# Cross-attention on one core: a GpSimd subtraction stops waiting for VectorE's rotation add, and a VectorE step moves one slot ahead

## The reference

```python
h = rmsnorm(x, norm_w)
q = rope((h @ Wq.T).reshape(B, Td, H, D), 0, D)
kv = (ctx @ Wkv.T).reshape(B, Te, 2, H, D)
k, v = rope(kv[:, :, 0], 0, D), kv[:, :, 1]
attn = softmax(einsum('bqhd,bkhd->bhqk', q, k) * D ** -0.5)
out = x + einsum('bhqk,bkhd->bqhd', attn, v).reshape(B, Td, d) @ Wo.T
```

## Time and profile before

| | |
|---|---|
| Time, median of 3 runs | 1491.78 us (1489.89 to 1495.62) |
| Profiled execution, its own time | 1495.62 us |
| Its span | 1493.8 us |
| Mean granted TensorE clock | 0.96 of full |
| Busy: PE, DVE, ACT, POOL | 87%, 78%, 60%, 59% |
| Longest groups on POOL and DVE | L1073 128 x 3096 ns; L1117 128 x 1936 ns |
| DMA packets | 310827, 148 GB/s |

### The profile page before, as it was taken

One profiled execution on the slowest core, in us unless ns is written; L12 is line 12 of the kernel. 1 busy time (PEld: TensorE's weight loads), 2 busy tenths in 40 slices (PEclk: granted clock), 3 DMA queues, 4 the chain that ended last, 5 costly groups with the idle time before them and its releaser, 6 DMA issues.

```text
span 1493.8 us, 34244 instructions
## 1 busy us (share of the span) xinstructions
PE 1297.5 (87%) x11592; PEld 715.1 (48%) x11592; DVE 1169.0 (78%) x1696; ACT 899.6 (60%) x1202; POOL 887.7 (59%) x738
## 2 busy tenths in 40 slices
PE   2787766799899999999899999999999999989997
PEld 1443332455455554555455555455545555545554
DVE  3755664788787888888788888888888888879874
ACT  2622333666566766766676666676667666756552
POOL 1234553567565666666666666666666666666551
PEclk9999896899999999999999999999999999999999
DMA  3433254677777777777777776777777777786642
GB/s 130 126 109 108 65 155 83 126 149 161 140 157 154 167 163 166 165 166 164 167 164 163 165 166 165 167 164 164 159 162 154 164 162 164 159 167 141 148 114 85
DMA packets 310827, 221.09 MB, mean 148 GB/s; under 512 B 230416, under 2 KB 284816, under 8 KB 302576
## 3 DMA queue, kind: packets, MB, share of 16 engines
q1 hardware_dynamic: 307984, 215.29, 64.1%
q10 hardware_dynamic: 2784, 5.05, 0.9%
HBM read 92.16 MB, written 43.65 MB: 91 GB/s over the span
## 4 chain that ended last, share of the span: by engine, by line
SPq 57%; issue 10%; PE 6%; DVE 4%; POOL 1%; DMA 1%; ACT 0%; DVEq 0%; ACTq 0%; POOLq 0%
SPq L813 24%; SPq L168 17%; SPq L829 4%; SPq L799 3%; SPq L857 3%; SPq L835 2%; PE a_ps L917 2%; PE b_ps L982 1%; PE a_ps L982 1%; DVE p_part L1117 1%; DVE maxima L1152 1%; POOL sin_part L1067 1%; SPq L862 1%; SPq L840 1%; SPq L853 1%
## 5 line engine op out<-in xcount | busy, mean ns | idle before, releaser
L1073 POOL TENSOR_TENSOR p_part<-probs,p_part 77x1536 f16<-77x1536 f32 x128 | 396.3, 3096 | 124.1 <-DVE q_rot L1147 107.9
L917 PE MATMUL a_ps<-h_t,wq 128*128 128x512 f16 x1536 | 378.4, 399 | 40.2 <-DMA h_t<-h_nat 30.7
L982 PE MATMUL b_ps<-wo,o_part 128*128 128x512 f16 x1464 | 337.1, 380 | 20.3 <-DVE o_part L1140 16.8
L1020 ACT ACTIVATE probs<-score_ps,scales 77x2048 f32<-77x2048 f32 x128 | 251.2, 1963 | 54.4 <-PE score_ps L903 54.2
L917 PEld LDWEIGHTS a_ps<-h_t,wq 128*128 128x128 f16 x1536 | 153.5, 102 | 246.6 <-DMA h_t<-h_nat 43.0
L1067 POOL TENSOR_TENSOR sin_part<-swapped,consts 128x512 f32<-128x512 f32 x128 | 162.8, 1272 | 145.9 <-DVE swapped L1135 145.9
L1117 DVE TENSOR_TENSOR p_part<-probs,p_part 77x512 f16<-77x512 f32 x128 | 247.8, 1936 | 0.0
L1034 ACT ACTIVATE p_part<-probs 77x2048 f16<-77x2048 f32 x128 | 242.9, 1898 | 0.0
L982 PEld LDWEIGHTS b_ps<-wo,o_part 128*128 128x128 f16 x1464 | 133.8, 98 | 173.0 <-DVE o_part L1140 25.1
L1152 DVE TENSOR_REDUCE maxima<-score_ps 128x16 f16<-128x1232 f32 x128 | 183.7, 1435 | 0.1
L1147 DVE TENSOR_TENSOR q_rot<-cos_part,sin_part 128x512 f32<-128x512 f32 x128 | 88.6, 692 | 108.7 <-POOL sin_part L1067 108.7
(11 more groups left out here) (107 smaller groups left out, 1832.7 us busy)
## 6 DMA issues: line engine op xcount, KB each, us to landing
q_stack<-q_part SPq DMA_DIRECT2D x756, 64.0 KB, 2.1
x_in<-x SPq DMA_DIRECT2D x32, 1024.0 KB, 5.9
res<-x SPq DMA_DIRECT2D x32, 1024.0 KB, 5.2
out<-res SPq DMA_DIRECT2D x64, 512.0 KB, 3.2
v_sb<-v_dram SPq DMA_DIRECT2D x32, 154.0 KB
k_stack<-k_hi_dram SPq DMA_DIRECT2D x64, 77.0 KB, 6.1
c_nat<-ctx SPq DMA_DIRECT2D x19, 256.0 KB, 2.8
v_dram<-v_row ACTq DMA_DIRECT2D x19, 256.0 KB, 2.1
```

What stands on the lines that cost most here:

```text
L917: mm = nc.tensor.matmul(a_ps[:, :], wq[:, w, k, g * P:(g + 1) * P], h_t[:, t.parity, h, k, :], start=(k == 0 and w == 0 and h == 0), stop= ...
L982: mm = nc.tensor.matmul(projection_bank(t, 0)[:, :], o_part[:, par, o, k, j * P:(j + 1) * P], wo[:, w, k, :], start=(k == 0 and o == 0 and ...
L1020: nc.scalar.activation(probs[:, g % 2, :, :], score_ps[0:S, :, :], ACT.Exp, scale=exp_scale[0:S, :]).then_inc(exped, 1)
L1073: nc.gpsimd.tensor_tensor(p_part[:, g % 2, 1, LO_V:J, :], probs[:, g % 2, LO_V:J, :], p_part[:, g % 2, 0, LO_V:J, :], ALU.subtract).then_i ...
```

## The change

There are two edits. On GpSimd, L1073 no longer waits for `q_full`; it still waits for `p_hi`. On VectorE, the values' low part leaves `g == 3`, where it stood between L1117 and L160, and becomes the last step of `g == 2`, behind the row maxima. Its wait, operands and semaphore stay.

```diff
@@ gpsimd
                 if t.has(4):
                     pool.wait_ge(p_hi, s - 3)
-                    if t.has(0):
-                        pool.wait_ge(q_full, s + 1)
                     nc.gpsimd.tensor_tensor(p_part[:, g % 2, 1, LO_V:J, :], probs[:, g % 2, LO_V:J, :],
                                             p_part[:, g % 2, 0, LO_V:J, :], ALU.subtract).then_inc(p_lo_p, 1)
@@ vector
-                if g == 3 and t.batch_ok(0):
-                    b, half, par = t.batch(0)
-                    dve.wait_ge(v_hi, b + 1)
-                    nc.vector.scalar_tensor_tensor(
-                        out=v_part[:, par, :, HD + 1:2 * HD + 1], in0=v_sb[:, par, :].rearrange("s (h d) -> s h d", d=HD),
-                        scalar=v_gain[0:S, :], in1=v_part[:, par, :, 0:HD], op0=ALU.mult, op1=ALU.subtract).then_inc(v_lo, 1)
-
                 if t.has(-7):
                     inp.low(dve, t)
@@
                     nc.vector.tensor_reduce(maxima[:, :, :].rearrange("p j q -> p q j"),
                                             score_ps[:, :, 0:J * S].rearrange("p q (j k) -> p q j k", k=S), AX.X, ALU.max).then_inc(max_red, 1)
+
+                if g == 2 and t.batch_ok(0):
+                    b, half, par = t.batch(0)
+                    dve.wait_ge(v_hi, b + 1)
+                    nc.vector.scalar_tensor_tensor(
+                        out=v_part[:, par, :, HD + 1:2 * HD + 1], in0=v_sb[:, par, :].rearrange("s (h d) -> s h d", d=HD),
+                        scalar=v_gain[0:S, :], in1=v_part[:, par, :, 0:HD], op0=ALU.mult, op1=ALU.subtract).then_inc(v_lo, 1)
```

## The result

The changed kernel takes 1622.8 us (median of 4, 1622.1 to 1623.74), the one before on the same chips 1492.8. The ratio is 1.087 (95% interval 1.085 to 1.089): slower, inside the stated range, 20 us above the forecast of 1603.

A forecast was written before the change was run, and what follows sets the result against it. SyncE's DMA queue was taken to bound the kernel at 38.5 us a batch. The changed batch, 8.79 + 8.79 + 10.94 + 13.26 = 41.8, gave 79 + 26 + 6 = +111 us on 1495.6: 1607, forecast 1603, range 1548 to 1745.

The forecast's parts named there:

- L1147 wins with the wait gone in g = 0, 1, 2: In these slots VectorE's L1147 starts before GpSimd's L1073 and holds it off; 0.13 us less a slot, 8.79 us.
- VectorE's circle: The chain L1147, L1073, L1059, L1117, L1134, back to L1147 sets a slot; 0.13 us shorter without the wait.
- the tie rival: L1073 also wins in g = 1 or 2, costing 4.5 us a batch more, 1742 us in all; chance 0.14.
- The loss in g = 3: L1073 starts ahead of L1147, which ends 2.89 us late; the slot costs 13.26 us with the clock loss.
- L1123 moved: At its new place in g = 2 VectorE's L1123 is blocked by L1073 and L1059; cost 1.36 us a batch.
- The hold over two GpSimd instructions: A blocked VectorE instruction stays blocked through the next GpSimd one; by the skill page g = 2 would take 1.09 less.
- The DMA queue hides 2.2 us a batch: SyncE's DMA issues set 38.5 us a batch, the engines alone need 36.3; losses up to the difference stay hidden.
- The clock: After TensorE idles near 3 us in g = 3, 3.40 us at half clock add 1.67 us.
- The six other places and slots 4, 5: Outside the 24 steady batches: six places at 4.4 us, 26 us, and two lost races at 2.9, 6 us.
- no race is lost: L1147 always gets in first; a batch of 37.3 us stays hidden by the DMA queue, 1490 to 1498; chance 0.13.
- The clock holds: TensorE's gap in g = 3 is too short to lower its clock; 1.67 x 31 us less, 1551; chance 0.09.
- The signs: Expected in the trace: L1138 near 3.6 us in g = 3, L1149 3.4, TensorE idle 3 us, then half clock.

The follow-up runs named there:

- the third experiment: Changed kernel with GpSimd's wait for q_full put back in g = 3 alone: 1.0094 of the kernel before, 1507 us.
- the first experiment: Changed kernel with GpSimd's wait for q_full put back, so only the move of L1123 is left: 1.0016 of the kernel before.
- the relief: Kernel before with four DMA issues a batch (v_sb, k_stack) moved from SyncE to ScalarE's queue: 0.9654, 1440 us; with L1123 moved too, 0.995, 1484 us.
- the filled gap: Changed kernel with 12 unread matmuls added in TensorE's 3.04 us gap in g = 3 of the hardware loop: 1.0509 of the kernel before, 1566 us.

## Why the prediction was right, step by step

- *L1147 wins with the wait gone in g = 0, 1, 2.* Right from slot 6 on. A slot takes 8.75 us (I said 8.79), bound by TensorE, for which L1125 waits. VectorE's circle was mis-sized: I let a held L1073 start only at the recorded end of L1147, 0.13 us earlier than before. In all 72 such slots of the 24 batches L1071 ends at t+3.64 or t+3.65, in place of t+3.93 before, so it gains 0.29. My lead of 0.13 us for `g` 0 to 2 was 0.14 to 0.27 as recorded. In the profiles of the seven kernels that drop the wait in some slots, the order of the two recorded starts decides all 868 units that have both steps: wherever the probabilities' low part is recorded as starting 0.02 us or more ahead of `q_rot` (133 units, 0.02 to 0.09), `q_rot` is 3.6 us; wherever it starts 0.14 or more behind, 0.69. Nothing fell between, so the threshold is no closer than that, and the tie rival (0.14) was not tested by a real tie.
- *The loss in g = 3.* L1138 3.57 us (I said 3.58), L1143 2.88 later (2.89). Right, and the third experiment shows it: with `g = 3` won, a batch is back at 38.58, and the rest of the change is hidden.
- *L1123 moved.* 3.35 us (3.4), `g = 2` 10.76 (10.94, too much by the 0.16 us that L1071 ends earlier than I had it). In the first experiment, with the later L1073, 3.64. Right. That the DMA queue hid it when it was alone is shown by the relief, where it costs 44 us.
- *The hold over two GpSimd instructions.* L1149 came free behind L1059, which ended at 877.08 in the rows above, and not at L1071's end, 875.96; so in all 24 batches. The rule of the Trainium skill, "SBUF — State Buffer" (summary for kernel authors), a block until the first one finishes, would have had 875.96; the trace does not agree, the hold is longer.
- *The DMA queue hides 2.2 us a batch.* Right in kind: the same 38.51 with the move, 36.93 with the relief. What the relief shows of the cover is 38.51 - 36.93 = 1.6 us, and not 2.2: I had 36.3 for the engines by themselves. The forecast hardly suffers from it: its sum over the 24 batches takes only the slots.
- *The clock.* The mechanism was right; its size is the term of the sum that was off. I took 1.67 us a batch (10.39 - 8.70 is 1.69) and 13.26 for `g = 3`; it took 13.56 and 15.24 in turn, mean 14.3, since the half clock lasts 3.4 us behind one gap and 6.8 behind the next. Over the forecast that is 1.04 us a batch, or 0.8 net of the slots that were shorter than forecast. In the 24 batches it makes 97 us where I had 79. "A second such stretch, 1.7 more" was my upper bound, and every other batch paid it.
- *The six other places and slots 4, 5.* I had 32 us; outside the 24 batches the span grew by 124.6 - 97.4 = 27. Together with the 18 us too few above, the span grew 14 us more than the 111 of the forecast. The rest of the 20 us is the spread of the executions: the profiled one was the slowest of its kernel before and the fastest after.
- *The rivals.* The end of "no race is lost" can be seen in the third experiment: with the race of `g = 3` taken out, a batch is 38.58, hidden as that rival had it. "The clock holds" fails: the filled gap gave back 2.2 us a batch. "A tie is lost" fails with the 92 short `q_rot` of the changed kernel.
- *The signs.* All came but one in size: L1071 was to be 0.6 us longer in three of four slots and is 0.4 longer.

What stays open: why a half clock follows a gap of 3.04 us for 6.8 us here and not at all there. It is no matter of the kernel alone: of the four executions with only the wait removed, three took 1550 to 1551 us at a mean clock of 0.944, and one 1565 us at 0.891.

## What to carry to other kernels

I wrote at the start that the engines meet only at semaphores. VectorE, with two operands in SBUF, and GpSimd meet once more: the one that starts first holds the other off. (The row maxima, L1143, whose data operand is in PSUM, keep their 1.44 us beside L1071.) A wait between them that looks needless may be what keeps a long instruction from starting a hair ahead of a short one on the path. Before taking it out, read from the trace which of the two would start first in every kind of slot, and by how much. A stall on the path can be paid twice if TensorE idles through it, once as time and once as clock. And slack elsewhere (here a DMA queue) can hide an edit that is alone, and not the same edit beside another: test edits with the cover taken away.

## What was not expected of the hardware

- The half clock behind a gap of 3.04 us lasted 6.8 or 3.4 us in the changed kernel, in turn from batch to batch. With only the wait removed (a batch of 40.4 us) it was 3.4 behind 18 of the 24 gaps, 6.8 behind two and absent behind four.
- Twelve useless matmuls in a gap of 3.04 us gave back 2.2 us a batch.
- A GpSimd instruction that is held off shows it as a longer duration (3.49 in place of 3.10), not as idle time, and so does VectorE's (3.57 in place of 0.69).
